# FiLM-FFN and mixture-of-experts kernel on one core: first token chunk written out, and its first two quarters split into halves together

## The reference, cut to what matters

```python
h1 = jnp.einsum('bth,efh->btef', x, w1) + b1
h1 = jax.nn.gelu(h1, approximate=False)
expert_outputs = jnp.einsum('btef,ehf->bteh', h1, w2) + b2
# x here is the output of the recurrence  h[t] = tanh(x[t] @ Wx + h[t-1] @ Wh + b)
```

## Time and profile before

| | us |
|---|---|
| median of 3 runs | 303.77 |
| all runs | 303.02, 303.77, 392.54 |
| profiled execution, first to last instruction (span) | 301.2 |
| TensorE busy in the profile | 264.4 (88%) |
| VectorE busy in the profile | 258.8 (86%) |
| ScalarE busy in the profile | 215.6 (72%) |

### The profile page before, as it was taken

How to read it: one execution, slowest core, us unless ns; L and a number is a source line. 1 busy time by engine, 2 the same in 40 slices (tenths; PEclk the granted TensorE clock), 3 DMA queues, 4 the chain that set the end, 5 groups by cost and what they waited for, 6 DMA issues and landing times.

```text
span 301.2 us, 8834 instructions
## 1 busy us (share of the span) xinstructions
PE 264.4 (88%) x2716; PEld 205.5 (68%) x2716; DVE 258.8 (86%) x635; ACT 215.6 (72%) x455; POOL 76.2 (25%) x148
## 2 busy tenths in 40 slices
PE   4969940049989999999999999999999999999994
PEld 4824440016956777778888788888777887888874
DVE  4888999989898897779988799887799988889885
ACT  6367899998842677767777676667566766689892
POOL 3367997000025413011302112212110311101000
PEclk9989976557999999999999999999999999999999
DMA  6990443101500000000000000000001000001000
GB/s 186 314 310 4 84 94 76 28 0 35 90 17 2 0 3 1 0 2 2 19 0 0 2 3 26 2 0 0 1 2 30 8 0 0 2 1 37 0 2 27
DMA packets 24031, 10.63 MB, mean 35 GB/s; under 512 B 13355, under 2 KB 22982, under 8 KB 24006
## 3 DMA queue, kind: packets, MB, share of 16 engines
q1 hardware_dynamic: 23470, 10.05, 13.6%
q10 hardware_dynamic: 536, 0.26, 0.3%
HBM read 6.11 MB, written 1.05 MB: 24 GB/s over the span
## 4 chain that ended last, share of the span: by engine, by line
PE 79%; DVE 16%; issue 1%; ACT 1%; DMA 1%; SPq 0%; DVEq 0%
PE bank L893 78%; DVE peak L706 3%; DVE big L728 3%; DVE peak L633 2%; DVE big L711 1%; DVE big L744 1%; PE bank L937 1%; DMA y_sb<-in_cond 1%; PE bank L1017 0%; DVE big L746 0%; DVE wyT L779 0%; DVE pkm L626 0%; DVE big L738 0%; DVE x_sb L759 0%; DVE q L700 0%
## 5 line engine op out<-in xcount | busy, mean ns | idle before, releaser
L893 PE MATMUL bank<-big,wt 128*128 128x384 f16 (+2 forms) x480 | 124.8, 336 | 0.6 <-DVE big L872 0.5
L893 PE MATMUL bank<-wt,big 128*128 (+1 forms) x1536 | 111.5, 219 | 0.1
L872 DVE TENSOR_TENSOR big<-big 128x384 f16<-128x384 f32 (+2 forms) x160 | 93.2, 585 | 20.5 <-ACT big L594 16.1
L893 PEld LDWEIGHTS bank<-wt,big 128*128 128x128 f16 x1536 | 97.9, 97 | 16.2 <-issue 0.2
L592 ACT ACTIVATE big<-bank,miscT 128x384 f32<-128x384 f32 (+2 forms) x160 | 96.2, 602 | 15.3 <-PE bank L893 8.2
L893 PEld LDWEIGHTS bank<-q,wxh 128*128 128x128 f32 x254 | 44.4, 189 | 17.4 <-issue 3.4
L893 PEld LDWEIGHTS bank<-big,wt 128*128 (+1 forms) x480 | 50.0, 117 | 4.8 <-issue 1.1
L580 ACT ACTIVATE q<-bank (+1 forms) x112 | 20.6, 184 | 38.7 <-PE bank L893 37.9
L404 POOL CAST big<-q 128x64 f16<-128x64 f32 x32 | 13.2, 413 | 129.0 <-ACT q L580 126.5
L868 DVE CAST big<-big 128x512 f16<-128x512 f32 (+2 forms) x104 | 38.6, 372 | 4.8 <-ACT big L592 3.9
L827 DVE SCALAR_TENSOR_TENSOR wyT<-bank,gates,wyT 128x128 f32<-128x128 f32 x128 | 39.8, 343 | 1.0 <-issue 0.6
(11 more groups left out here) (165 smaller groups left out, 320.0 us busy)
## 6 DMA issues: line engine op xcount, KB each, us to landing
wnat<-in_w SPq DMA_DIRECT2D x8, 512.0 KB, 7.7
x_sb<-in_x SPq DMA_DIRECT2D x4, 256.0 KB, 4.3
out_block<-wyT SPq DMA_DIRECT2D x15, 64.0 KB
wn<-in_w_gate ACTq DMA_DIRECT2D x1, 192.0 KB, 4.9
wn<-in_w_up SPq DMA_DIRECT2D x1, 192.0 KB, 5.6
wn<-in_w_down SPq DMA_DIRECT2D x1, 192.0 KB, 5.7
b_in<-in_b SPq DMA_DIRECT2D x12, 4.0 KB
wt<-wyT SPq DMA_TRANSPOSE x8, 3.0
```

Source lines behind the costliest of these rows:

```text
L872: V.tensor_tensor(g_lo[:, par, f, 0:w], g32[:, f, 0:w], g_hi[:, par, f, 0:w], ALU.subtract).then_inc(g_lo_done, 1)
L893: return nc.tensor.matmul(o, l, r, start=start, stop=stop, skip_group_check=True)
```

## The change

`chunks` writes out all four pairs of chunk 0; chunks 1 to 4 stay as they were. `is_last` replaces the test for "written out and not the first pair", so that the work which belongs behind the last pair of chunk 4 is not done in chunk 0. On VectorE, in chunk 0, the cast and the subtraction of quarter 0 are no longer made in slot 0: in slot 1 one cast and one subtraction handle quarters 0 and 1 together (2 x 256 elements per partition), once the Gelu of quarter 1 is there, and each counter goes up by 2. Quarters 2 and 3 are as before.

```diff
--- before.py
+++ after.py
@@ -235,8 +235,10 @@
         def chunks(eng, pair):
 
 
-            for c in range(CH):
-                pair(c, 0, c > 0)
+            for e2 in range(E // 2):
+                pair(0, e2, e2 > 0)
+            for c in range(1, CH):
+                pair(c, 0, True)
                 with eng.Fori(1, E // 2 - (c == CH - 1)) as e2:
                     pair(c, e2, True)
             pair(CH - 1, E // 2 - 1, True)
@@ -244,6 +246,10 @@
         def is_first(e2):
 
             return isinstance(e2, int) and e2 == 0
+
+        def is_last(c, e2):
+
+            return c == CH - 1 and isinstance(e2, int) and e2 == E // 2 - 1
 
         def added_before(c, e2, par):
 
@@ -583,7 +589,7 @@
 
                     if first and s == 5 and c > 0:
                         take_gates(c - 1)
-                    if isinstance(e2, int) and not first and s == 3:
+                    if is_last(c, e2) and s == 3:
                         take_gates(c)
                     act.wait_ge(hid_mm, slot + 1)
                     bias = miscT[:, bass.ds(e2 * 2 * NF + s, 1)]
@@ -853,7 +859,7 @@
                         take_logits(c)
                     if first and s == 7 and c > 0:
                         add_b2(c - 1)
-                    if isinstance(e2, int) and not first and s == 6:
+                    if is_last(c, e2) and s == 6:
                         add_b2(c, 2)
                     if first and s == 2:
                         dve.wait_ge(logit_sb, c + 1)
@@ -863,14 +869,21 @@
                         dve.wait_ge(top_done, 2 * START[c + 1] // P)
                     if first and s == 6:
                         mix(c)
-                    if f not in HI_SCALAR[c]:
+                    if c == 0 and f == 1:
                         dve.wait_ge(g32_done, slot + 1)
-                        V.tensor_copy(g_hi[:, par, f, 0:w], g32[:, f, 0:w]).then_inc(hi_v, 1)
+                        V.tensor_copy(g_hi[:, par, 0:2, 0:w], g32[:, 0:2, 0:w]).then_inc(hi_v, 2)
                         dve.wait_ge(hi_v, hi_made(c, e2, s, False))
-                    else:
-                        dve.wait_ge(g_hi_done, hi_made(c, e2, s, True))
-                    V.tensor_tensor(g_lo[:, par, f, 0:w], g32[:, f, 0:w], g_hi[:, par, f, 0:w],
-                                    ALU.subtract).then_inc(g_lo_done, 1)
+                        V.tensor_tensor(g_lo[:, par, 0:2, 0:w], g32[:, 0:2, 0:w], g_hi[:, par, 0:2, 0:w],
+                                        ALU.subtract).then_inc(g_lo_done, 2)
+                    elif c > 0 or f > 1:
+                        if f not in HI_SCALAR[c]:
+                            dve.wait_ge(g32_done, slot + 1)
+                            V.tensor_copy(g_hi[:, par, f, 0:w], g32[:, f, 0:w]).then_inc(hi_v, 1)
+                            dve.wait_ge(hi_v, hi_made(c, e2, s, False))
+                        else:
+                            dve.wait_ge(g_hi_done, hi_made(c, e2, s, True))
+                        V.tensor_tensor(g_lo[:, par, f, 0:w], g32[:, f, 0:w], g_hi[:, par, f, 0:w],
+                                        ALU.subtract).then_inc(g_lo_done, 1)
                     if first and s == 2:
                         find_top(c)
                     if first and s == 3:
@@ -1138,9 +1151,9 @@
                         transpose_gates(c - 1)
                     if first and c > 0 and s == 6:
                         mix_b2(c - 1)
-                    if isinstance(e2, int) and not first and s == 2:
+                    if is_last(c, e2) and s == 2:
                         transpose_gates(c)
-                    if isinstance(e2, int) and not first and s == 4:
+                    if is_last(c, e2) and s == 4:
                         mix_b2(c)
 
             pe.wait_ge(h32_done, FIRST_STEPS)
```

## The result

The changed kernel takes 299.77 us (median of 4 runs, 298.88 to 300.45), the kernel before 303.39 (median of its three earlier runs and one made beside the changed kernel, 302.59). The ratio is 0.9897 with a 95% interval of 0.987 to 0.9924: 1.0% less, 2.3 to 3.9 us. It leaves out one slow run of the kernel before, 392.54 us, and so is not the quotient of the two medians. The forecast was 299.4 in a range of 298.0 to 302.0, and "within 2%".

The account below looks back on a forecast made before the run. The prediction took TensorE to bound the kernel, slowed in chunk 0's loop by its own issuing. -5.10 (written out), +0.59 (slot 4) and +0.10 (slot 12) gave -4.4 us: 299.4 from 303.77, range 298.0 to 302.0.

Parts of the forecast that it names:

- What bounds the kernel: From chunk 1's start the chain of waits is 167.18 us on TensorE alone, so TensorE's gain in chunk 0 stays.
- Pairs 1 to 3 at the speed of pair 0: Chunk 0's loop pairs, written out: six experts at 3.06 us, 18.36 against 23.46, a gain of 5.10 us.
- TensorE's own issuing: Chunk 0's loop: 0.27 to 0.34 us lost before the recurrence matmul to TensorE's issue with register addresses, not the tanh.
- VectorE keeps up; the merge makes room: Chunk 0: VectorE needs 2.60 us an expert merged, 2.87 unmerged, against TensorE's 3.06.
- The merged half, hidden with 0.2 to spare: Quarter 0's later low half lets TensorE start at 3.31 us; it asks at 3.52, so the wait is hidden.
- Pair 0: Chunk 0's first pair: slot 4 starts 0.59 us later for the merged low half; 0.1 more at slot 12.
- Sum: Whole kernel: -5.10 + 0.59 + 0.10 = -4.4 us, a span of 296.8 us and a time of 299.4.
- Pacing by the merged half: Rival: VectorE or the merged half paces the written-out pairs, 300.0 to 302.4 us, centre 301; chance 0.20.
- the slow cast: The merged split cast might run at the rate of the one 977 ns cast, 1.30 us in place of 423 ns.
- "slower" case: Rival: a split cast of 1.30 us brings low halves 0.88 us later, 304.3 us; decides from 0.2 of lateness; chance 0.03.
- No gain: Rival: gaps belong to the recurrence matmul or code supply makes new ones; 303.5 or 304.4 us; chance 0.06.
- More is gained: Rival: slot 4 hardly later and chunk 1's first pair less held up; 298.6 down to 297.5 us; chance 0.11.

Follow-up runs that it names:

- e1: The changed kernel with the merge turned off, chunk 0 still written out: 298.70 us, ratio 0.9884 against the kernel before.
- e2: The changed kernel with the loops put back and the merge kept: 303.63 us, ratio 1.0034 against the kernel before.
- e5: The changed kernel with TensorE back in its loop for pairs 1 to 3 of chunk 0, ScalarE and VectorE written out: 302.84 us, ratio 1.0006.
- e4: The changed kernel with pairs 1 to 3 of chunk 0 written out on TensorE alone, ScalarE and VectorE in loops: 300.07 us, ratio 0.9929.
- e9: The changed kernel with every merged cast made twice, the second behind the first: 302.54 us (one run), chunk 0 28.02 us.

## Why the prediction was right, and where it was off

- **What bounds the kernel.** Right. Chunk 1 took 0.11 us more in the changed kernel and the rest the same, so what chunk 0 gained stayed gained.
- **Pairs 1 to 3 at the speed of pair 0.** Right: the floor of 18.36 us became 18.88 (106.96 to 125.84). 0.24 of the rest is the wait at slot 12, 0.14 slot 25, 0.1 the wait for the last tanh in front of chunk 1. Without slot 12, which the sum has as a term of its own, the gain is 4.82 us for the 5.10 reckoned: the floor allowed for no wait at all. e1 confirms it without the merge.
- **"TensorE's own issuing".** Mostly right: 3.90 of 4.77 us. The step excluded a wait for the tanh by one load, that of slot 9, which came half a microsecond behind it; in slots 12, 20 and 28 the tanh seems to have had a part. It said nothing of ScalarE's and VectorE's own register work. That cost 0.85 us with TensorE in its loop (e2 against e5) and 0.87 with TensorE written out (e4 against the changed kernel). The forecast did not suffer, since the change writes out all three.
- **VectorE keeps up; the merge makes room.** The first half held, even without the merge: e1 runs with VectorE 96% busy. The merged form costs more than reckoned: 0.53 us from its cast to its subtraction and not 0.46, though the cast itself (0.42 to 0.46) is as fast as the flat one. The split form kept the pace of the flat one, 0.43 us for 0.42. The Trainium skill (VectorE: DVE Perf Modes, "Mode 2×_2P") has a copy within SBUF at two results a clock where its outermost dimension is even; the trace agrees.
- **The merged half, hidden with 0.2 to spare.** Right: an estimate of 0.19 by e9, of 0.11 by the timeline.
- **Pair 0.** Right in kind, too small: 0.72 us at slot 4 for the 0.59 reckoned, since the cast started 0.10 behind the Gelu's end (101.95 + 0.47 = 102.42, cast 102.52) and the subtraction 0.54 behind the cast. Slot 12 waited 0.24 for the 0.10 reckoned. The step had VectorE save 0.27 us by each of the two merges of pair 0 and begin pair 1's adds 0.35 sooner. In the second expert it first idled 0.23 us, at 105.93, for the Gelu of slot 5, for which a merged cast has to wait; the adds began 8.25 us into chunk 0 (at 108.86), where they had begun at 8.20 (109.38). The longer merged form, 0.07 us each time, is the smaller part.
- **Sum.** -3.85 us in chunk 0 for -4.4. The mis-sized terms are the gain of the loop pairs, 0.28 too large, the wait at slot 4, 0.13 too small, and the wait at slot 12, 0.14 too small: together 0.55. The span of 296.9 us beside the 296.8 of the forecast is luck: the unchanged part ahead of chunk 0 happened to be 0.57 us shorter. The ratio's interval, 2.3 to 3.9 us, holds 3.85 and not 4.4.
- **The rivals.** Pacing by the merged half and the slow cast did not come; all eight merged casts ran at 0.42 to 0.46 us. The "slower" case had its mechanism right and its condition wrong: e9, with the low half 0.53 us later, lost 2.8 us in chunk 0. The 0.2 us of lateness from which on it decides agrees with the 0.19 worked out from e9. "No gain" fell with the first 0.80 us slot. "More is gained" did not come either: slot 4 was 0.72 us later and chunk 1 no shorter.

## What to carry to other kernels

Compare a loop's slots with the same slots in written-out form, start to start: a busy share of 98% hid a fifth of the time. Register addresses cost time here in most of the 256-wide slots with a step (0.27 us on a slot of 0.80) and none in the 384-wide ones of 1.13. So write out the narrow chunks first; a wide one gives back only its jumps, 0.5 us for chunk 1. That it is the width that decides was not tried by itself. Merging two small operations saves their overhead but makes the first result as late as the second; ask who waits for the first, and do it only where the engine that it relieves is the one that paces.

## What the runs showed of the hardware that was not expected

ScalarE lost time once in its written-out code. Its timeline in the changed kernel, and TensorE's next recurrence load:

```profile
119.22 0.18 ACT L586 ACTIVATE q<-bank 128x16 f32<-128x16 f32 x1 [0.21 <-PE bank L906]
119.56 0.47 ACT L598 ACTIVATE big<-bank,miscT 128x256 f32<-128x256 f32 x1 [0.16 <-issue]
```

```profile
120.53 0.30 PEld L906 LDWEIGHTS bank<-q,wxh 128*128 128x128 f32 x2 [0.15 <-ACT q L586]
```

The Gelu of slot 23 starts 0.34 us behind the tanh's start, where 0.11 is usual (114.69, 114.80), with 0.16 put down to issue; the next tanh is late, and TensorE's load waits 0.15. All ten kernels with ScalarE written out show this gap, 0.34 to 0.35 us at this same Gelu; where ScalarE kept its loop it is absent. Slot 25 took 0.94 us in place of 0.80 in eight of the ten. The other two are e5, whose TensorE is in its loop, and e9, where TensorE had already waited at slot 24 and slot 25 took 0.80. The row of e9:

```profile
122.00 0.47 ACT L598 ACTIVATE big<-bank,miscT 128x256 f32<-128x256 f32 x1 [0.16 <-issue]
```

The packets of code in the page's part on queues do not go with the gap: e5 has it with 14 packets, as many as the kernel before, and e4 (ScalarE in its loop) has 15, as many as the changed kernel, and not the gap.

```profile
q8 instruction: 15, 0.25, 0.4%
```

The Trainium skill (Runtime: NRT & Kernel Launch, "Instruction fetch mechanics") has the crossing of a code block's border "mostly hidden". Whether this gap is such a crossing was not tried; its cause stays open.
